# First attention of a two-layer kernel: value products of four heads at once, packed two heads to a 32-row group, one flip per batch; division and normalize on GpSimd

## What is computed

```
q, k, v = W x + b          # per-channel projections, x normalized, k and v from the context
q, k    = rotary(q), rotary(k)
scores  = einsum('bdhn,bdhm->bhnm', q, k) / sqrt(8)
prob    = softmax(scores, axis=-1)
x       = einsum('bhnm,bdhm->bdhn', prob, v)
out     = Wm x + bm        # added to the residual
```

## Time and profile before

| | us |
|---|---|
| three timed runs | 486.32, 487.55, 487.72 |
| median | 487.55 |
| profiled execution, span from first to last instruction | 485.7 |
| first attention, from the first scores to the last flip of values | about 36 to 188 |

### The profile page before, as it was taken

How to read it: one execution, slowest core, us unless ns; L and a number is a source line. 1 busy time by engine, 2 the same in 40 slices (tenths; PEclk the granted TensorE clock), 3 DMA queues, 4 the chain that set the end, 5 groups by cost and what they waited for, 6 DMA issues and landing times.

```text
span 485.7 us, 8153 instructions
## 1 busy us (share of the span) xinstructions
PE 422.1 (87%) x2754; PEld 264.6 (54%) x2754; DVE 347.6 (72%) x948; ACT 175.4 (36%) x230; POOL 60.0 (12%) x132
## 2 busy tenths in 40 slices
PE   5269998999999987999999999999878777596896
PEld 4125554555555543366666667677556555364444
DVE  7895888888887858466545626676876777868693
ACT  1105444455454451233343433343354444341001
POOL 3222324233242110000000000000000000000000
PEclk9777999999999998999999999999998889876997
DMA  6552335466364031000000000233125554630011
GB/s 214 151 164 70 97 118 158 133 216 196 121 197 123 4 118 43 0 2 0 1 0 0 1 1 11 62 90 111 53 78 164 163 160 126 180 89 1 1 43 43
DMA packets 63408, 42.53 MB, mean 88 GB/s; under 512 B 4625, under 2 KB 61201, under 8 KB 63377
## 3 DMA queue, kind: packets, MB, share of 16 engines
q1 hardware_dynamic: 62080, 41.24, 28.4%
q10 hardware_dynamic: 1296, 0.89, 0.7%
HBM read 27.76 MB, written 14.16 MB: 86 GB/s over the span
## 4 chain that ended last, share of the span: by engine, by line
issue 52%; PE 23%; DVE 14%; POOL 4%; DMA 3%; SPq 1%; ACT 1%; POOLq 0%; DVEq 0%
PE psum L501 7%; PE psum L469 3%; PE psum L489 3%; DVE mx L1114 3%; PE psum L456 2%; PE psum L816 2%; POOL parts L315 1%; PE psum L800 1%; DVE stats L1089 1%; PE psum L587 1%; DMA qstk<-mT 1%; DMA wa<-in_wa 1%; PE psum L725 1%; DVE rope_ab L1103 1%; DMA kstk<-stack_scratch 1%
## 5 line engine op out<-in xcount | busy, mean ns | idle before, releaser
L857 ACT ACTIVATE prob<-psum 128x1024 f32<-128x1024 f32 x64 | 65.6, 1024 | 89.8 <-PE psum L489 89.7
L1114 DVE TENSOR_REDUCE mx<-psum 128x2 f32<-128x512 f32 x128 | 84.1, 682 | 17.9 <-PE psum L469 16.9
L1334 DVE SCALAR_TENSOR_TENSOR xall<-psum,comb,xall 128x256 f32<-128x256 f32 x128 | 53.1, 477 | 41.5 <-PE psum L612 41.1
L612 PE MATMUL psum<-wdn,act 128*128 128x256 f32 x320 | 75.5, 379 | 0.6 <-DVE xall L1331 0.6
L599 PE MATMUL psum<-xnT,wup 128*128 128x512 f32 x160 | 76.0, 598 | 0.0
L612 PEld LDWEIGHTS psum<-wdn,act 128*128 128x128 f32 x320 | 60.7, 190 | 25.9 <-issue 19.1
L501 PE MATMUL psum<-prob,vt 128*32 128x256 f32 x512 | 69.0, 389 | 0.7 <-DVE pvT L1128 0.5
L900 ACT ACTIVATE rel<-psum 128x512 f32<-128x512 f32 x40 | 23.9, 597 | 96.2 <-PE psum L599 96.2
L469 PE MATMUL psum<-kstk,qstk 128*128 128x256 bf16 x256 | 50.8, 283 | 3.4 <-DVE mx L1114 3.3
L315 POOL TENSOR_TENSOR parts<-qk_rest,parts 128x512 bf16<-128x512 f32 x15 | 17.3, 1156 | 244.2 <-ACT parts L925 236.5
L958 ACT ACTIVATE prob<-psum 128x1024 f32<-128x1024 f32 x32 | 32.7, 1024 | 31.4 <-PE psum L710 30.4
(11 more groups left out here) (149 smaller groups left out, 484.7 us busy)
## 6 DMA issues: line engine op xcount, KB each, us to landing
qstk<-stack_scratch SPq DMA_DIRECT2D x32, 256.0 KB, 3.2
kstk<-stack_scratch SPq DMA_DIRECT2D x64, 128.0 KB, 3.3
stack_scratch<-parts SPq DMA_DIRECT2D x32, 192.0 KB, 2.3
stack_scratch<-parts SPq DMA_DIRECT2D x32, 128.0 KB, 2.2
wup<-in_wup SPq DMA_DIRECT2D x4, 640.0 KB, 4.8
wdn<-in_wdn SPq DMA_DIRECT2D x4, 640.0 KB, 5.6
stack_scratch<-parts SPq DMA_DIRECT2D x32, 64.0 KB, 1.9
ctx<-in_ctx SPq DMA_DIRECT2D x10, 128.0 KB, 2.2
```

The lines of the kernel that those rows point to most:

```text
L612: last = nc.tensor.matmul(y_banks(y)[:, j // 2, (j % 2) * D:(j % 2 + 1) * D], act2[n % 2][:, j * P:(j + 1) * P], wdn[:, BLOCKS[g], :], sta ...
L857: nc.scalar.activation(prob[k % 2][:], exp_buf(k).rearrange("p a n -> p (a n)"), ACT.Exp, scale=SCALE).then_inc(exp_done, 1)
L1114: nc.vector.tensor_reduce(mx[:, half, :, 4 * s + p4:4 * s + p4 + 1], bank.rearrange("n (b m) -> n b m", b=2), AX_X, ALU.max).then_inc(misc ...
L1334: last = nc.vector.scalar_tensor_tensor(out=xall[:, b, :], in0=src, scalar=comb[:, b, e:e + 1], in1=xall[:, b, :], op0=ALU.mult, op1=ALU.add)
```

## The change

- `pv` now takes two pairs, that is four heads, at a time, at spots 3, 7, 11 and 15. Its eight matmuls go round the four 32-row groups of the bank, where the four of before stayed in two groups. Two heads share one group: of the low one the weights are columns 8 to 40 of a 40-wide row of vt, of the high one columns 0 to 32, so that their values fall on neighbouring rows, and their sums on two more; the products of the low and the high one add up in PSUM. A whole batch then fits into one bank.
- DVE flips once per batch, at spot 1 of the next slot, and takes one reciprocal. GpSimd does the two multiplications (`divide`), DVE transposes back at spot 4 (`flip_back`).
- v+wm moves from spot 4 to spot 7. In slots 1 to 6 ScalarE copies the values (`values_in`, after the exponential of pair 4), and `add_output` on DVE waits for that (v_taken).
- The normalization of batch b+3 in slots 0 to 4 moves from DVE to GpSimd, and GpSimd's loop is written out.
- There are four prob buffers, and some semaphore counts change. At the end the ones of vt are set for the second attention, which reads columns 8 to 40.

SP's code is the same; the count for which it waits is that of v+wm in its new place.

The core of the diff:

```diff
-            u += [("v+wm",)] if (m or wm) and spot == 4 else []
+            u += [("v+wm",)] if (m or wm) and spot == 7 else []
...
-            def pv(b, par, k):
-                pe.wait_ge(exp_done, b * PAIRS + k + 2)
-                if k % 4 == 0:
-                    pe.wait_ge(pv_free, 2 * b + 2 + k // 4)
-                for s in range(2):
-                    j, g = 2 * (k % 2) + s, k // 2
-                    for mb in range(2):
+            def pv(b, par, t):
+
+                pe.wait_ge(exp_done, b * PAIRS + 2 * t + 3)
+                if t == 0:
+                    pe.wait_ge(pv_free, b + 2)
+                g, low = t // 2, t % 2 == 0
+                for mb in range(2):
+                    for j in range(4):
+                        k, s = 2 * t + j // 2, j % 2
                         last = nc.tensor.matmul(
-                            pv_bank(1)[32 * j:32 * j + 32, (g % 2) * D:(g % 2 + 1) * D],
-                            vt[par][:, mb, 2 * k + s, :],
-                            prob[k % 2][:, (2 * s + mb) * D:(2 * s + mb + 1) * D],
-                            start=(mb == 0), stop=(mb == 1))
+                            pv_bank(1)[32 * j:32 * j + 32, g * D:(g + 1) * D],
+                            vt[par][:, mb, 4 * t + j, 8:40] if low else vt[par][:, mb, 4 * t + j, 0:32],
+                            prob[k % 4][:, (2 * s + mb) * D:(2 * s + mb + 1) * D],
+                            start=(low and mb == 0), stop=(not low and mb == 1), skip_group_check=True)
                 last.then_inc(pv_done, 1)
...
+            def values_in(b0, b, flags):
+
+                n = a_index(flags, ("v+wm",))
+                act.wait_ge(misc_full, a_base(b) + n + 1)
+                act.wait_ge(pv_done, b * QUADS)
+                nc.scalar.copy(vt[(b0 + 1) % 2][:, :, :, 8:16],
+                               misc(a_base(b0) + n)[:, 0:D].rearrange("m (a h d) -> m a h d", a=2, d=HD)
+                               ).then_inc(v_taken, 1)
...
+            def normalize(b):
+
+                nc.gpsimd.tensor_scalar(xn[b % 2][:], xall[:, b, :], nmean[:, b:b + 1], rstd[:, b:b + 1],
+                                        ALU.add, ALU.mult).then_inc(xn_ready, 1)
+
+            def divide(b):
+
+                pool.wait_ge(den_ready, b + 1)
+                if b:
+                    pool.wait_ge(o3_ready, b)
...
+                for g in range(2):
+                    last = nc.gpsimd.tensor_tensor(
+                        o[:, g], cells[:, g, :, 0:2 * HD].rearrange("p n (t d) -> p n t d", d=HD),
+                        by[:, g].unsqueeze(3).broadcast_to((P, 8, 2, HD)), ALU.mult)
+                last.then_inc(o2_ready, 1)
...
+                if pqk:
+                    if b >= 1:
+                        pool.wait_ge(misc_free, a_base(b - 1) - 1)
+                    normalize(b + 3)
+                if b < NB - 2:
+                    rest(b + 2, b % 2)
+                if b:
+                    divide(b - 1)
+                if b < NB - 2:
+                    third(b + 2, b % 2)
...
+            def flip(b):
+
+                dve.wait_ge(pv_done, b * QUADS + QUADS)
+                nc.vector.transpose(pvT[0][:], pv_bank(1)).then_inc(pv_free, 1)
+                dve.wait_ge(pv_free, b + 3)
+                nc.vector.reciprocal(den[0][:].rearrange("p (x t) -> p x t", t=2),
+                                     pvT[0][:].rearrange("p (x r) -> p x r", r=32)[:, :, 2 * HD:2 * HD + 2]
+                                     ).then_inc(den_ready, 1)
+
+            def flip_back(b):
+
+                dve.wait_ge(o2_ready, b + 1)
+                nc.vector.transpose(o3[:], o2[:]).then_inc(o3_ready, 1)
```

More of the change, by code:

```diff
@@ L28 @@
 MAX_ROW = 46
+VROW = 40
+QUADS = 4
 PAIRS = 8
@@ L82, in build @@
         rstd = sb("rstd", [P, NB])
+        nmean = sb("nmean", [P, NB])
         rs_v = sb("rs_v", [P, 64])
@@ L545, in slot @@
                     step = spot // 2
-                    if spot % 2:
-                        pv(b, par, step)
+                    if spot % 4 == 3:
+                        pv(b, par, spot // 4)
+                    elif spot % 2:
+                        pass
                     elif step < PAIRS - 1:
@@ L886, in slot @@
                         second_parts(b + 2, b0 % 2)
+                    if 0 < shape < NB - 1 and k == 4:
+                        values_in(b0, b, a_flags(shape))
             slot(0, 0, 0)
@@ L1034, in _ @@
                 negate(len(PROLOGUE) + FIRST_MAX.index(PAIRS * (half + 1) - 1) + 1, half)
[L1036 to L1041, removed]
+            def normalize(b):
[5 more added lines that the diff above has]
+                    pool.wait_ge(o3_ready, b)
+                cells = pvT[0][:].rearrange("p (g n r) -> p g n r", g=2, r=32)
+                o = o2[:].rearrange("p (n g t d) -> p g n t d", g=2, t=2, d=HD)
+                by = den[0][:].rearrange("p (g n t) -> p g n t", g=2, t=2)
+                for g in range(2):
[3 more added lines that the diff above has]
+                last.then_inc(o2_ready, 1)
+            pool.wait_ge(stats_ready, 1)
+            for b in range(NB):
+                wm, m, pqk = flags = a_flags(b)
+                if pqk:
[8 more added lines that the diff above has]
+                    third(b + 2, b % 2)
                 if m:
@@ L1047, in slot @@
                     negate(a_base(b) + a_index(flags, ("max", 7, 1)) + 1, 1)
[L1049 to L1056, removed]
+            divide(NB - 1)
             with pool.Fori(0, 4) as i:
@@ L1123, in add_output @@
                                                       op0=ALU.add, op1=ALU.add)
[L1125 to L1134, removed]
-                o = o2[:].rearrange("p (n g d) -> p g n d", g=4, d=HD)
-                for g in range(2):
-                    last = nc.vector.tensor_tensor(
-                        o[:, 2 * i + g], cells[:, 8 * g:8 * g + 8, 0:HD],
-                        den[i][:, 8 * g:8 * g + 8].unsqueeze(2).broadcast_to((P, 8, HD)), ALU.mult)
-                steps.then(last)
-                if i == 1:
-                    nc.vector.transpose(o3[:], o2[:]).then_inc(o3_ready, 1)
+            def flip(b):
[8 more added lines that the diff above has]
+                nc.vector.transpose(o3[:], o2[:]).then_inc(o3_ready, 1)
             for i in range(2):
                 steps.then(nc.vector.memset(vt[i][:], 0.0))
-                last = nc.vector.memset(vt[i][:, :, :, HD:HD + 1], 1.0)
-                last.then_inc(pv_free, 1)
+                halves = vt[i][:].rearrange("m a (g t j) r -> m (a g) t j r", g=2, t=2)
+                nc.vector.memset(halves[:, :, 0, :, 24:25], 1.0)
+                nc.vector.memset(halves[:, :, 1, :, 17:18], 1.0).then_inc(pv_free, 1)
             dve.wait_ge(x_in[0], 16)
@@ L1189, in slot @@
                 wm, m, pqk = flags = a_flags(shape)
-                if pqk:
-                    normalize(b + 3, (b0 + 1) % 2)
                 n = 0
                 for spot in range(2 * PAIRS):
-                    if spot in (7, 15):
-                        flip(b, spot // 8)
+                    if spot == 1 and shape:
+                        flip(b - 1)
+                    if spot == 4 and shape:
+                        flip_back(b - 1)
                     for use in a_uses(spot, *flags):
@@ L1231, in _ @@
             with dve.Fori(0, 2) as i:
-                steps.enter(i, 8)
                 for b0 in (1, 2):
                     slot(b0, i, 1)
-            steps.leave(2)
             for b in (5, 6, 7):
                 slot(b, 0, b)
-            divide(NB - 1, 1)
+            flip(NB - 1)
+            flip_back(NB - 1)
+            for i in range(2):
+                nc.vector.memset(vt[i][:, :, :, 16:17], 1.0)
             def spread(small, big, n):
```

47 lines of the change are left out of this document (24 added, 23 removed).

## The result

| | us (range, runs) | to before, 95% |
|---|---|---|
| before | 486.94 (481.69 to 487.72, 4) | |
| after | 502.21 (500.89 to 503.78, 4) | 1.035 [1.0282, 1.0419] |

The account below looks back on a forecast made before the run. Behind a busy TensorE it saw two latency chains per slot, SP's DMA queue deciding half A. Slots 1 to 4 +8.7, slot 0 +1.5, start -1.5, clock +3.0: +11.7, about 499 us, 2.4% slower; range 487 to 511.

Parts of the forecast that it names:

- The step that decides, half A: Mark 4 to mark 0 of a slot: SP's list, held by the later v+wm, lengthens it from 9.63 to 13.3 us.
- the sum: All terms over the whole kernel: +8.7 us, with the clock's 3.0 +11.7, span from 485.7 to 497.4.
- Half B: Mark 0 to the next mark 4: shrinks from 9.99 to 8.7 us, limited by DVE's order and the maxima's DMA.
- The clock: TensorE at half rate after new idle stretches: 0.6 us per slot taken, 3.0 in all, bounds 0 to 2 per slot.
- The rival with longer drops: Clock falls for longer, 2 us on each of five slots instead of 0.6: +7, 506 to 510; chance 0.12.
- The value products: On TensorE, a pv of two pairs costs 1.0 us, like one pair before: 4 us less in each of eight slots.
- The rival without overlap: Value products do not overlap four ways: each pv 2.0 us, +2.0 per slot over seven slots, about 513; chance 0.06.
- DVE and GpSimd: Per slot DVE loses about 3.5 us, GpSimd gains a normalize and two multiplications, 1.6 together, taken as hidden.
- The multiplications' stall: On DVE, one multiplication took most of its pair's 1.36 us beside GpSimd's 1.16 us operation; the move removes this.
- Start, slots 5 to 7: Ahead of slot 0's mark 4: -1.5 us; slots 5 to 7, without context load: 0, bounds -4 and +2.
- TensorE's saving comes through: Faster if SP's list does not hold half A: A 9.8, B 8.7, about 480 us; chance 0.13.

Follow-up runs that it names:

- e1: Changed kernel with SP's six DMAs of the parts put ahead of the wait for v+wm and the context load: 468.60 us, 0.9688 to before.
- e2: Kernel before with only v+wm moved from spot 4 to spot 7: 505.31 us, 1.0438 to before.
- e3: Changed kernel with 64 small overwritten matmuls ahead of the scores at mark 0 in slots 0 to 4: 488.43 us, 1.0067 to before.
- e4: Changed kernel with the two loops inside pv exchanged, so a row group's two matmuls follow each other: 499.51 us, 1.0274 to before.
- e9: e8 with the context load of slots 0 to 4 issued by ScalarE after the exponential of pair 4, not by SP: 472.16 us, 0.9718 to before.
- e8: e1 with the projection of q moved from spot 9 to spot 11: 472.01 us, 0.973 to before.

## Why the prediction was right, and where it was off

- **The step that decides, half A.** Right in place, kind and size in slots 3 and 4: predicted load at 4.3, DMA at 10.8, half 13.3; measured 4.42 and 4.39, 11.13 and 10.99, 13.37 and 13.33. Shown by e1 (wait out of the way, loss gone) and e2 (wait alone, loss there).
- **Slots 1 and 2** took 15.61 and 14.68, 3.7 more than the sum had. In slot 2 SP's first three issues of parts took 2.76 us instead of 1.46. In slot 1 the parts' last DMAs were issued at 71.15 + 1.43, and the fetch that waits for them at 75.59, 3.0 us later, against 1.3 in slot 3:

```profile
71.15 1.43 SPq L358 DMA_DIRECT2D stack_scratch<-parts  x3
75.59 0.37 SPq L364 DMA_DIRECT2D qstk<-stack_scratch  x1
```

  The kernel before has longer halves A in these slots too (10.56, 10.17), and e2 as well (15.01, 13.75). With the same SP list slot 1 took 13.87 in e3 and 13.86 in e4, so part of it changes from run to run. I took SP's list from one slot and multiplied; its length in four slots was in the trace. Why these DMAs land later there stays open.
- **Half B.** Predicted 8.7 and 0.6 of clock, 9.3; measured 9.3 to 10.3. Both terms were off, in opposite ways. At full clock it is 8.0 (e1, e3): the DMA goes out at 6.0, as worked out (6.2; the reciprocal took 0.35 and not 0.25), but takes 2.08 to the scores where I carried the 2.51 of half A, whose DMA flies beside the stack fetches.
- **The clock** was the term most under-sized: 3.0 us in the sum, 8.2 by e3 (48.3 less 40.1). It is shown by e3 that the idle time ahead of mark 0 is the cause. I supposed that part of the drop passes while TensorE waits. So it does in slots 1 and 4, where the drop lasts 6.8 us and begins 3.6 and 1.8 ahead of mark 0; in slots 0, 2 and 3 it lasts 3.4 and begins between 0.5 ahead of mark 0 and 1.0 behind it. But 2.9 us or more of it lie behind mark 0 in every slot, and the price of 1.3 to 2.3 us a slot is two to four times my 0.6, once even above my bound of 2. The Trainium skill (TensorE: Matmul & The Clock Gate, "Part 1") states that half rate is the default and activity lifts it; e3, where useless matmuls keep the later ones at full rate, agrees. The rival with longer drops (2 us a slot, 506 to 510) was thus nearer to the clock's price than the forecast was.
- **The value products.** Predicted 1.0 us for two pairs; measured 1.00 from the start of pv to the next matmul (1.07 to its end), TensorE 15.0 us busy a slot in e1 against 18.8. The rival without overlap is out. That the gain hides behind the latency chains was right: they gave half B only 1.0 us in sum.
- **DVE and GpSimd.** DVE lost 2.8 us a slot (68.01 to 56.79 in four), 3.5 predicted; GpSimd's share grew by 1.0, 1.6 predicted: the new rows are 0.55 and twice 0.39:

```profile
132.99 0.55 POOL L1060 TENSOR_SCALAR xn<-xall,nmean,rstd 128x256 f32<-128x256 f32 x1
...
134.62 0.77 POOL L1072 TENSOR_TENSOR o<-pvT,den 128x128 f32<-128x128 f32 x2
```

  That they are hidden held. The multiplications' stall of the earlier trace rows is gone, one multiplication had taken 1.2 us beside such an operation and 0.22 alone, and row maxima beside GpSimd's 1.16 us operations keep their mean of 0.67, against 0.69 elsewhere. This agrees with the Trainium skill (SBUF — State Buffer, "Who interferes with whom"), by which a VectorE instruction with at most one input in SBUF, outside the modes that use two ports, does not contend with GpSimd.
- **Start, slots 5 to 7.** -2.5 and -2.4 where the sum had -1.5 and 0, inside the bounds given.
- **The rivals.** "TensorE's saving comes through" named its own condition, SP's stretch out of the way, and foresaw about 480 for it. e1 made the condition true and reached 469: its halves are 9.4 and 8.0 instead of 9.8 and 8.7, with the DMA of half A at 7.3 after mark 4 as that rival had it, and a flight of 2.1 instead of 2.5.

By terms, measured less predicted: half A of slots 1 to 4 +3.8, the halves B of these slots +1.6 (the clock's +1.05 each, with 0.65 each given back by the shorter flight), slot 0 +0.1, start and late slots -3.4, the rest of the program +2.0, the last of which is within what that stretch varies by. Together 4.1 of the 4.2 between the spans of 497.4 and 501.6. The forecast was 3.2 us under the median, and some of that nearness is luck: in the five slots it was 5.5 us too low, and the start and the late slots, 3.4 too high, made up for most of it.

## What to carry to other kernels

When an instruction is moved later, follow every in-order queue in which someone waits for it, the DMA issuer's first, and list what stands behind that wait: here nearly 4 us of matmul time saved in each slot did not show, and one load at the head of a list cost 4 us in each of five slots. If an issue must wait, put ahead of it what need not. A wait moved to another engine's list, as in e9, holds up that list instead. And price an idle stretch of TensorE at its length plus what the half-rate time behind it costs; adding filler matmuls is a quick experiment for that part.

## What the runs showed of the hardware

- After idle stretches of 2.2 us (e2) and 4.1 us (the changed kernel) TensorE ran at the lower of its two levels, 1.2 instead of 2.4 GHz (granted clock 0.50 instead of 1.00), for 3.4 to 6.8 us (pv 1.94 instead of 1.07). 64 matmuls of 128x128, 3.74 us in all, put into the stretch (e3) kept it at full rate, and that was worth 1.3 to 2.3 us a slot.
- Matmuls with 32 weight columns overlap by how many of the four row groups are in use close by: starts come in fours (four groups: the changed kernel, e4) or twos (two groups: the kernel before), 0.22 us from one set to the next at 256 columns of f32, whatever the order within a pv.
- The small DMA of the maxima takes 2.0 to 2.1 us from issue to the waiting matmul when it goes alone (half B of the changed kernel and e1), 2.1 to 2.9 right behind three stack fetches of 512 KB in all (2.24 in slot 3 of the changed kernel, 2.61 in e8), and once 3.4 (slot 1 of e1).
- GpSimd's price by size, f32, in the changed kernel: 128x512 1.16 us, 128x256 with two scalars 0.55, 128x128 0.39, 128x16 0.22.
